# A fused four-layer kernel: the scan's preparation folded in two pieces, keys turned one step later, and unread bf16 matmuls on TensorE in the first part

## The chip, the cores and the metric

The kernel runs on 1 core of one Trainium2 chip. The metric is the device time of one execution in microseconds. The kernel before took 1473.23 us (median of 3 runs, 1469.16 to 1474.96).

## The reference

Eight sequences of 512 tokens with 128 channels go through four layers, each followed by a residual and a layer norm:

```
x = layernorm(x + attention(x))          # 16 heads of 8, causal, q and k layer-normed per head
x = layernorm(x + soft_moe(x))           # 8 experts x 64 slots; softmax over experts (dispatch) and over all slots (combine)
x = layernorm(x + delta_rule_block(x))   # q,k,v = silu(x @ W), l2-normed; recurrent state per head; then a gated MLP
x = layernorm(x + ternary_mlp(x))        # three gelu/silu layers of width 512
```

The first two layers and the preparation of the third (projections, norms, and the folding of four time steps of the delta rule into one) are the first part, up to about 885 us. The scan over time with both MLPs is the second part; the change doesn't touch it.

## The kernel before

The kernel is written by hand, one instruction stream for each engine, with counting semaphores between them. The order of work on each engine is the order in which the code issues it.

The first part is a software pipeline over the 8 sequences. One turn of it is a **slot**, `slot(b, moe, front, tail, ...)`, which works on up to five sequences at once: `b` is in attention (scores, exponentials, products with v), `moe` = b-1 in the expert layer, `front` = b+1 has its q, k, v projected and the maxima of its scores taken, `tail` = b-2 is normed and projected for the third layer, `pre` = b-3 has its heads normed for the scan, and `folded` = b-4 has its time steps folded. So `folded` is there in slots 4 to 7, `front` in slots 0 to 6; slots 3 to 6 are the loop.

Inside a slot the attention's steps `(gg, jt)` (head group, key tile) run from (0, 0) to (4, 3) on TensorE, and the other sequences' work is threaded between them at fixed steps. What matters here, with the lines of the profile:

- **Tops and exponentials of the expert logits.** TensorE makes eight blocks of logits `L0..L3`, `M0..M3` (L962, L966). VectorE takes each one's row maximum (`top`, L1709), and only then can ScalarE take its exponential (L1294, with `accum_out`). L0 to L2 come at the slot's start, L3 and M0 at step (0, 2), M1 and M2 at (0, 3), M3 at (1, 0).
- **`fold_heads`** (VectorE, L1787 to L1807) is a generator of ten steps on the tiles of `late`: products of pairs (L1793, three instructions), a sum (L1796), a fold and a subtraction (L1798, L1799), and two rounds of product, sum, subtraction (L1803, L1805, L1806). `sum_scores` (L1811) follows. In a slot, `finish_heads` runs all of it between the tops L2 and L3. SyncE's queue stores the result to DRAM (`store_heads`, L555) and only behind it replicates the next sequence's q and k (L512, then L517).
- **`norms(front)`** (L1669, L1670, the reciprocal root, L1672) gives `qk_n`. At `QK_TURNED = (1, 3)` TensorE transposes q and k (L871), ScalarE writes each twice (`take_qk_T`: L1294 into `arena` and `hilo`), and GpSimd makes the low parts (L699). ScalarE's `take_products`, on which the products of step (2, 0) wait, comes in step (2, 0) between two exponentials.
- **Maxima.** `scores_for_maxima` works off 22 units of scores of `front` at the slot's end: matmuls of 32 rows (L903) and a bf16 mask added by a matmul of `ident_b` with `mask_qk` (L906). VectorE reduces each unit (L1683). There are two pairs of PSUM banks, so unit k waits until unit k-2 is reduced. Units 14 to 21 are 512 columns wide; units 17 to 21 come behind all other PE work of the slot. Then the maxima are transposed (L871), cast (L1690) and sent by DMA into `qr` (L525), which the next slot's scores need.

`ps` bank 6 holds the attention's products `pvT`; `ring` hands banks 4, 5, 7 to everything else. `idle` matmuls don't exist in this kernel.

Of the kernel before, what the change touches and what calls it, by code (L numbers as in the profile page):

```python
# [21 lines left out]
ACT = mybir.ActivationFunctionType  # L22
X = mybir.AxisListType.X

P = 128
B, S, D = 8, 512, 128
NT = S // P
# [20 lines left out]
CREDIT = 1  # L48
# [93 lines left out]
def build(nc, A, out, taps=None):  # L142
    ctx = ExitStack()
    with ctx:
# [529 lines left out]
        def _(g):  # L674
# [81 lines left out]
            def slot(i, front, pre):  # L756
                for gg in range(NG):
                    for jt in range(NT):
                        if i is not None:
                            causal(i, gg, jt)  # L760
                        if front is not None:
                            if (gg, jt) == (0, 1):
                                squares(front)
                            if (gg, jt) == QK_TURNED:
                                low_parts(front)
                        if pre is not None and (gg, jt) == (2, 1):
                            squares_heads(pre)
                if front is not None:
                    place_v(front)
                    add_bias(front)  # L770
                if pre is not None:
                    scale_heads(pre)
                    score_products(pre)
# [73 lines left out]
        def _(pe):  # L847
# [34 lines left out]

            def transpose_qk(b, turn):
                pe.wait_ge(qk_normed, CREDIT + b + 1)
                transposes("qT", turn, [qk_n[:, t, 0:D] for t in range(NT)]).then_inc(f_ready, 1)
                transposes("kT", turn, [qk_n[:, t, D:2 * D] for t in range(NT)]).then_inc(f_ready, 1)

            def scores_for_maxima(b, first, end):
# [4 lines left out]
                for k in range(first, end):  # L893
# [11 lines left out]
                    for bank in banks:  # L905
                        last = pe.matmul(bank[:, :, it * P:w], ident_b[:, :],  # L906
                                         mask_qk[:, :].unsqueeze(1).broadcast_to([P, len(gs), P]), start=False, stop=True)
                    last.then_inc(s_ready, 1)

            def transpose_maxima(b, turn):  # L910
# [114 lines left out]
            def slot(b, moe, front, tail, before):  # L1025
# [4 lines left out]
                if moe is not None:  # L1030
                    for t in range(3):
                        token_logits(moe, turn, t)
                if b is not None:
                    pe.wait_ge(max_placed, CREDIT + (b + 1) * 64)
                for gg in range(NG + 1):
                    for jt in range(NT):
                        if b is not None and gg < NG:
                            scores(b, gg, jt)
                        if front is not None:
                            if (gg, jt) in ((0, 0), (0, 1)):  # L1040
                                project_qkv(front, turn, 2 * jt)
                                project_qkv(front, turn, 2 * jt + 1)
                            if (gg, jt) == QK_TURNED:
                                transpose_qk(front, turn)
                        if moe is not None:
# [45 lines left out]
                if moe is not None:  # L1091
                    expert_hidden(moe, turn, 2)
                    expert_hidden(moe, turn, 3)
                if tail is not None:
                    transpose_x2(tail, turn)
                if b is not None:
# [25 lines left out]
                if front is not None:  # L1122
                    maxima_to(NX)
                    transpose_maxima(front, turn)
# [11 lines left out]
            turn_weights(6, [raw_slot[:, j, :] for j in range(4)]).then_inc(slot_turned, 1)  # L1136
            transpose_qk(0, first)
            pe.wait_ge(slot_taken, 1)
            scores_for_maxima(0, 0, NX)
            transpose_maxima(0, first)  # L1140
# [140 lines left out]
        def _(act):  # L1281
# [26 lines left out]

            def take_qk_T(b):


                act.wait_ge(split_done, CREDIT + b)
                act.wait_ge(split_stored, CREDIT + b * 96)
                for j, n in enumerate("qk"):
                    for dst in (qk_T[:, j, :], hilo[:, j, 0, :]):
                        r = take(F, f"{n}T", b, dst, lambda p: p, ACT.Identity, scale=qk_gb[:, 2 * j:2 * j + 1],
                                 bias=qk_gb[:, 2 * j + 1:2 * j + 2])
                    r.then_inc(f_act, 1)

# [68 lines left out]
            def slot(b, moe, front, tail):  # L1388
# [5 lines left out]
                for gg in range(NG):  # L1394
                    for jt in range(NT):
# [5 lines left out]
                        if front is not None:  # L1401
                            if (gg, jt) in ((0, 0), (0, 1)):
                                take_qkv(front, 2 * jt)
                                take_qkv(front, 2 * jt + 1)
                            if (gg, jt) == QK_TURNED:
                                take_qk_T(front)
                        if moe is not None:
# [42 lines left out]
            act.wait_ge(w_final, 1)  # L1450
            take_qk_T(0)
            act.wait_ge(setup_pool, 8)
# [127 lines left out]
        def _(v):  # L1580
# [243 lines left out]
            def slot(b, moe, front, tail, pre, folded):  # L1824
                tops = None
                if moe is not None:
                    for t in range(3):
                        top(moe, "L", t)
                    if folded is not None:
                        finish_heads(folded)  # L1830
                    top(moe, "L", 3)
                    top(moe, "M", 0)
                    tops = slot_tops(moe)
                if front is not None:
                    norms(front, (lambda: next(tops, None)) if tops else None)
                if moe is not None:
# [3 lines left out]
                    v.reciprocal(z_inv, z_sum).then_inc(inv_ready, 1)  # L1840
                    apply_x1(moe)
                if b is not None:
                    attend(b, 0)
# [157 lines left out]

QK_TURNED = (1, 3)

# [33 lines left out]
```

## Time and profile before

| | |
|---|---|
| median of 3 runs | 1473.23 us |
| profiled execution, own time | 1466.32 us |
| its span | 1464.6 us |
| busy: PE, DVE, ACT, POOL | 1144.2, 969.0, 618.8, 448.4 us |
| mean granted TensorE clock | 0.84 of full speed |

The profiled execution's time is its span and 1.7 us around it. Durations come from this one execution. The digits of the page's second part give for each fortieth of the span (36.6 us) how busy an engine was, in tenths; PEclk is the clock that TensorE was granted, where 1.00 is 2.4 GHz and 0.50 is 1.2 GHz; in between, a slice holds stretches of both:

```
PE   2778898897988988989897602049898898988997
DVE  3616436564686685866847758888888898888221
PEclk7576797998988979889699755569898989898898
```

### The profile page before, as it was taken

What the parts mean: (1) busy time and instruction counts of PE and PEld (TensorE: products, weight loads), DVE (VectorE), ACT (ScalarE), POOL (GpSimd) and SP (SyncE); (2) the same over time, 40 slices, a digit from 0 to 9 for tenths busy, and PEclk for the clock granted to TensorE, in tenths of its full rate; (3) what the DMA queues carried; (4) which work ended last, traced back from release to release, by engine and by line L of the source; (5) the groups of instructions that cost most, each with busy time, mean ns of one, the idle gap of its engine ahead of it and who ended that gap; (6) DMA issues with size and microseconds to landing.
All of it is one profiled execution on the core that took longest, in us unless ns stands there. A gap on an engine that the chain in (4) does not pass through costs nothing.

```text
span 1464.6 us, 18213 instructions
## 1 busy us (share of the span) xinstructions
PE 1144.2 (78%) x5332; PEld 579.5 (40%) x5332; DVE 969.0 (66%) x2391; ACT 618.8 (42%) x1170; POOL 448.4 (31%) x460
## 2 busy tenths in 40 slices
PE   2778898897988988989897602049898898988997
PEld 1334355453544535535345302014344343443443
DVE  3616436564686685866847758888888898888221
ACT  1061642827537256174374302025344453444542
POOL 2031210302233043341341351153443534435210
PEclk7576797998988979889699755569898988989898
DMA  4111030220322322132103373101022020210000
GB/s 103 65 45 65 1 101 9 59 80 26 104 57 74 87 61 100 40 94 87 35 21 84 83 187 104 45 7 46 8 53 61 8 53 8 53 29 0 22 7 8
DMA packets 85335, 79.83 MB, mean 55 GB/s; under 512 B 42768, under 2 KB 62864, under 8 KB 83216
## 3 DMA queue, kind: packets, MB, share of 16 engines
q1 hardware_dynamic: 85264, 79.01, 19.7%
q8 instruction: 29, 0.48, 0.1%
q14 instruction: 42, 0.34, 0.1%
HBM read 43.45 MB, written 35.00 MB: 54 GB/s over the span
## 4 chain that ended last, share of the span: by engine, by line
PE 61%; DVE 19%; issue 7%; ACT 7%; POOL 2%; SPq 1%; DMA 1%; ACTq 0%; DVEq 0%; POOLq 0%
PE ps L1192 14%; PE ps L1178 9%; PE ps L871 5%; PE ps L933 5%; PE ps L903 5%; DVE arena L1683 4%; PE ps L906 3%; PE ps L922 3%; ACT arena L1332 3%; PE ps L962 2%; PE ps L1184 2%; PE ps L982 2%; ACT arena L1294 2%; PE ps L992 2%; PE ps L966 2%
## 5 line engine op out<-in xcount | busy, mean ns | idle before, releaser
L1294 ACT ACTIVATE arena<-ps 128x512 f32<-128x512 f32 (+2 forms) x200 | 110.1, 573 | 333.4 <-PE ps L871 213.6
L1683 DVE TENSOR_REDUCE arena<-ps 128x2 f32<-128x1024 f32 (+3 forms) x176 | 194.9, 1125 | 56.2 <-PE ps L906 53.5
L1192 PE MATMUL ps<-arena,late 128*128 128x512 f32 x512 | 225.6, 592 | 0.0
L1332 ACT ACTIVATE arena<-ps 128x1024 f32<-128x1024 f32 (+3 forms) x256 | 169.9, 716 | 34.3 <-PE ps L922 32.5
L721 POOL TENSOR_SCALAR_AFFINE_SELECT arena<-arena 128x512 f32<-128x512 f32 x128 | 86.2, 676 | 299.9 <-ACT arena L1332 299.1
L1178 PE MATMUL ps<-arena,late 128*128 128x512 f32 x256 | 135.3, 689 | 12.4 <-ACT arena L1464 12.4
L1192 PEld LDWEIGHTS ps<-arena,late 128*128 128x128 f32 x512 | 96.2, 190 | 115.8 <-issue 115.5
L871 PE MATMUL ps<-ident,arena 128*128 128x128 f32 (+1 forms) x640 | 108.8, 315 | 37.6 <-ACT arena L1294 12.2
L903 PE MATMUL ps<-kr,qr 32*128 32x512 f32 (+3 forms) x512 | 110.2, 481 | 32.3 <-issue 20.1
L1464 ACT ACTIVATE arena<-ps,f_s 128x512 f32<-128x512 f32 x128 | 87.3, 688 | 70.2 <-PE ps L1192 46.4
L933 PE MATMUL ps<-arena 128*32 128x512 f32 (+3 forms) x1024 | 98.2, 468 | 23.0 <-ACT arena L1294 23.0
L798 POOL TENSOR_TENSOR arena<-arena 128x512 f32<-128x512 f32 x64 | 81.3, 1270 | 99.1 <-ACT e_w L1514 99.1
L871 PEld LDWEIGHTS ps<-ident,arena 128*128 128x128 f32 (+1 forms) x640 | 78.9, 155 | 75.4 <-ACT arena L1294 19.7
L1464 ACT ACTIVATE arena<-ps 128x512 f32<-128x512 f32 x96 | 56.2, 597 | 103.2 <-PE ps L1184 70.9
L922 PE MATMUL ps<-qr,kr 32*128 32x256 f32 (+3 forms) x512 | 73.4, 437 | 23.8 <-ACT arena L1332 17.7
L1722 DVE RECIPROCAL arena<-ps 128x16 f32<-128x16 f32 x32 | 8.2, 257 | 122.0 <-PE ps L871 121.5
L1178 PEld LDWEIGHTS ps<-arena,late 128*128 128x128 f32 x256 | 55.2, 222 | 84.3 <-issue 71.5
L903 PEld LDWEIGHTS ps<-kr,qr 32*128 32x128 f32 x512 | 51.9, 227 | 84.7 <-DVE arena L1683 46.4
L922 PEld LDWEIGHTS ps<-qr,kr 32*128 32x128 f32 x512 | 34.1, 193 | 116.7 <-ACT arena L1332 88.9
L1709 DVE TENSOR_REDUCE arena<-ps 128x1 f32<-128x512 f32 x64 | 43.6, 689 | 46.6 <-PE ps L962 35.8
L713 POOL TENSOR_TENSOR arena<-arena,bias_o 128x512 f32<-128x512 f32 x8 | 10.1, 1267 | 208.2 <-DVE arena L1620 208.2
L808 POOL TENSOR_TENSOR arena<-arena 128x512 f32<-128x512 f32 x32 | 40.7, 1273 | 104.3 <-ACT arena L1464 104.2
(164 smaller groups left out, 1978.0 us busy)
## 6 DMA issues: line engine op xcount, KB each, us to landing
scan_d<-late SPq DMA_DIRECT2D x64, 138.0 KB, 2.9
qr<-q_rep SPq DMA_DIRECT2D x8, 1024.0 KB, 5.6
kr<-k_rep SPq DMA_DIRECT2D x8, 1024.0 KB, 7.9
arena<-scan_d SPq DMA_DIRECT2D x12, 552.0 KB, 7.0
q_rep<-hilo SPq DMA_DIRECT2D x24, 256.0 KB, 3.0
k_rep<-hilo SPq DMA_DIRECT2D x24, 256.0 KB, 3.9
proj_d<-arena SPq DMA_DIRECT2D x8, 768.0 KB, 5.1
late<-proj_d SPq DMA_DIRECT2D x8, 768.0 KB, 4.4
```

Of the source, the lines that this page charges most:

```text
L721: g.affine_select(out=block, in_=block, compare_op=ALU.is_ge, fill=0.0, base=0, pattern=[[0, 4], [1, P]], channel_multiplier=-1).then_inc( ...
L798: g.tensor_tensor(o_m[half][r][:, :, :, 0:HD], state[h][:, cs, :, :], qc[:, cs, r, :].unsqueeze(2).broadcast_to([P, HALF, HD, HD]), ALU.mult)
L871: last = pe.transpose(bank[0:src.shape[1], k * P:(k + 1) * P], src, ident[:, :])
L903: pe.matmul(bank[:, j, :], qr[rows, gg, it * P:(it + 1) * P], kr[rows, gg, 0:w], start=(j == 0), stop=False)
L922: last = pe.matmul(ps[:, 2 * (k % 2) + n, 0:S - jt * P], kr[rows, gg, jt * P:(jt + 1) * P], qr[rows, gg, jt * P:S], start=True, stop=True)
L933: last = pe.matmul(bank[32 * h4:32 * h4 + 32, jt * P:S], v_aug[:, jt, 4 * gg + h4, :], prob[:, gg % 2, h4, p_off[jt]:p_off[jt] + S - jt * ...
L1178: return pe.matmul(ps[:, ring2.bank(use), :], w, src, start=True, stop=True)
L1192: last = pe.matmul(ps[:, ring2.bank(f"{n}{c}"), :], w[:, k, c * P:(c + 1) * P], src[:, k, :], start=(k == 0), stop=(k == HC - 1))
L1294: return act.activation(dst, src(ps[:, bank, :]), func, **kw)
L1332: act.activation(prob[:, gg % 2, 2 * pr:2 * pr + 2, p_off[jt]:p_off[jt] + w], ps[:, bank:bank + 2, 0:w], ACT.Exp).then_inc(p_taken, 1)
L1464: return act.activation(dst, src(ps[:, ring2.bank(use), :]), func, **kw)
L1683: v.tensor_reduce(heads[:, 2 * pr:2 * pr + 2, gs[0]:gs[-1] + 1], ps[:, 2 * (k % 2):2 * (k % 2) + 2, 0:len(gs) * w].rearrange("p q (n w) -> ...
```

## The change

Five edits, all in the first part. (1) In slots with `folded`, the first 4 of `fold_heads`' steps stay between the tops L2 and L3; the others and `sum_scores` go behind `apply_x1(moe)`. (2) `QK_TURNED` becomes `Q_TURNED = (1, 3)` and `K_TURNED = (2, 0)`: TensorE, ScalarE and GpSimd do the keys one step later. (3) A helper `idle_matmuls` writes products into `ps` bank 6 that nobody reads: two ahead of each of the units 17 to 21, four ahead of the transposition of the maxima, two ahead of the wait for `max_placed` at a slot's start. (4) The 22 maxima units ahead of slot 0 have two each ahead of them. (5) In the last slot 24 stand ahead of `transpose_x2`.

```diff
                         if front is not None:
                             if (gg, jt) == (0, 1):
                                 squares(front)
-                            if (gg, jt) == QK_TURNED:
+                            if (gg, jt) == K_TURNED:
                                 low_parts(front)
...
-            def transpose_qk(b, turn):
-                pe.wait_ge(qk_normed, CREDIT + b + 1)
-                transposes("qT", turn, [qk_n[:, t, 0:D] for t in range(NT)]).then_inc(f_ready, 1)
-                transposes("kT", turn, [qk_n[:, t, D:2 * D] for t in range(NT)]).then_inc(f_ready, 1)
+            def transpose_qk(b, turn, j):
+                if j == 0:
+                    pe.wait_ge(qk_normed, CREDIT + b + 1)
+                transposes(("qT", "kT")[j], turn, [qk_n[:, t, j * D:(j + 1) * D] for t in range(NT)]).then_inc(f_ready, 1)
...
+            def idle_matmuls(n, bank=6):
+                for _ in range(n):
+                    pe.matmul(ps[:, bank, :], ident_b[:, :], mask_qk[:, :].unsqueeze(1).broadcast_to([P, 4, P]),
+                              start=True, stop=True)
...
                     for t in range(3):
                         token_logits(moe, turn, t)
+                    if b is not None:
+                        idle_matmuls(2)
                 if b is not None:
                     pe.wait_ge(max_placed, CREDIT + (b + 1) * 64)
...
-                            if (gg, jt) == QK_TURNED:
-                                transpose_qk(front, turn)
+                            if (gg, jt) == Q_TURNED:
+                                transpose_qk(front, turn, 0)
+                            if (gg, jt) == K_TURNED:
+                                transpose_qk(front, turn, 1)
...
                 if tail is not None:
+                    if moe is None:
+                        idle_matmuls(24)
                     transpose_x2(tail, turn)
...
                 if front is not None:
-                    maxima_to(NX)
+                    while x_at < NX:
+                        idle_matmuls(2)
+                        maxima_to(x_at + 1)
+                    idle_matmuls(4)
                     transpose_maxima(front, turn)
...
-            scores_for_maxima(0, 0, NX)
+            for k in range(NX):
+                idle_matmuls(2)
+                scores_for_maxima(0, k, k + 1)
             transpose_maxima(0, first)
...
-                            if (gg, jt) == QK_TURNED:
-                                take_qk_T(front)
+                            if (gg, jt) == Q_TURNED:
+                                take_qk_T(front, 0)
+                            if (gg, jt) == K_TURNED:
+                                take_qk_T(front, 1)
...
                     if folded is not None:
-                        finish_heads(folded)
+                        o_fold = Order(v, wy_done, DVE_WY, folded, CREDIT)
+                        folds = fold_heads(folded, o_fold)
+                        advance(o_fold, folds, 4)
                     top(moe, "L", 3)
...
                     apply_x1(moe)
+                    if folded is not None:
+                        advance(o_fold, folds, DVE_WY + 1)
+                        sum_scores(folded)
...
-QK_TURNED = (1, 3)
+Q_TURNED, K_TURNED = (1, 3), (2, 0)
```

## Rows read from the trace of the kernel before

**Rows 1.** Chain of waits in time: starts of slots 2, 3, 4, 5 (start, us)

```profile
243.44 1.88 PE ps L871 x8
333.33 1.88 PE ps L871 x8
...
425.12 1.88 PE ps L871 x8
...
520.75 1.88 PE ps L871 x8
```

**Rows 2.** Timeline of DVE, slot 5: start, duration; brackets: idle before, who ended it

```profile
530.21 0.69 DVE L1803 TENSOR_TENSOR late<-late 128x512 f32<-128x512 f32 x1
...
534.15 2.11 DVE L1806 TENSOR_TENSOR late<-late 128x256 f32<-128x256 f32 x1
536.38 1.49 DVE L1811 TENSOR_REDUCE late<-late 128x160 f32<-128x1280 f32 x1
537.79 1.28 DVE L1709 TENSOR_REDUCE arena<-ps 128x1 f32<-128x512 f32 x2
...
558.01 0.26 DVE L1722 RECIPROCAL arena<-ps 128x16 f32<-128x16 f32 x1 [7.56 <-PE ps L871]
```

**Rows 3.** Timeline of ACT, slot 5

```profile
538.58 0.69 ACT L1294 ACTIVATE arena<-ps,arena 128x512 f32<-128x512 f32 x1 [3.68 <-DVE arena L1709]
...
550.62 0.78 ACT L1294 ACTIVATE arena<-ps,qk_gb 128x512 f32<-128x512 f32 x1
```

**Rows 4.** Timeline of PE, slot 2, then slot 5

```profile
280.53 3.84 PE L982 MATMUL ps<-arena 128*128 128x128 f32 x32
...
533.41 1.13 PE L962 MATMUL ps<-slot_T,arena 128*128 128x512 f32 x2
...
539.41 2.08 PE L966 MATMUL ps<-arena,slot_T 128*128 128x512 f32 x2 [2.70 <-ACT arena L1294]
...
554.93 1.37 PE L933 MATMUL ps<-arena 128*32 128x512 f32 x8 [2.11 <-ACT arena L1294]
...
563.31 3.83 PE L982 MATMUL ps<-arena 128*128 128x128 f32 x32
```

**Rows 5.** Timeline of PE, late units of slot 5; logits at the slot's start

```profile
522.64 3.90 PE L962 MATMUL ps<-slot_T,arena 128*128 128x512 f32 x6
...
605.72 0.50 PE L903 MATMUL ps<-kr,qr 32*128 32x512 f32 x2 [0.40 <-DVE arena L1683]
...
606.85 0.79 PE L903 MATMUL ps<-kr,qr 32*128 32x512 f32 x2 [0.41 <-DVE arena L1683]
607.58 0.39 PE L906 MATMUL ps<-mask_qk,ident_b 128*128 128x128 bf16 x2
```

**Rows 6.** Timeline of DVE, late units of slot 5

```profile
607.74 8.53 DVE L1683 TENSOR_REDUCE arena<-ps 128x2 f32<-128x1024 f32 x7
```

**Rows 7.** Chain of waits: two bf16 matmuls of 512 columns, unit 0 and slot 5

```profile
45.06 0.96 PE ps L906 x2
...
584.30 0.54 PE ps L906 x2
```

**Rows 8.** Windows: PE, PEld, DVE, ACT, POOL busy (x), PEclk, DMA share, GB/s

```profile
43.90:72.60 28.70, 25.97 (x108) 11.30 (x108) 24.31 (x22) 0.00 (x0) 0.00 (x0) 0.50 0.00 1
...
606.80:620.40 13.60, 11.80 (x39) 5.63 (x40) 11.54 (x15) 1.20 (x2) 11.02 (x10) 0.50 0.07 20
```

**Rows 9.** Timeline of SP's queue, slot 5

```profile
538.05 4.72 SPq L555 DMA_DIRECT2D scan_d<-late  x8
555.87 1.88 SPq L512 DMA_DIRECT2D q_rep<-hilo  x3
...
572.17 0.40 SPq L517 DMA_DIRECT2D qr<-q_rep  x1
```

**Rows 10.** Timeline of ACT, slot 7

```profile
729.79 0.69 ACT L1294 ACTIVATE arena<-ps,arena 128x512 f32<-128x512 f32 x1 [4.44 <-DVE arena L1709]
```

**Rows 11.** Timeline of PE, slot 9

```profile
835.86 1.11 PE L871 MATMUL ps<-ident,arena 128*128 128x128 f32 x4 [9.40 <-DVE arena L1620]
```

More of the change, by code:

```diff
@@ L1136, in _ @@
             turn_weights(6, [raw_slot[:, j, :] for j in range(4)]).then_inc(slot_turned, 1)
-            transpose_qk(0, first)
+            transpose_qk(0, first, 0)
+            transpose_qk(0, first, 1)
             pe.wait_ge(slot_taken, 1)
-            scores_for_maxima(0, 0, NX)
+            for k in range(NX):
+                idle_matmuls(2)
+                scores_for_maxima(0, k, k + 1)
             transpose_maxima(0, first)
@@ L1307, in take_qkv, with take_qk_T @@
                 act.activation(v_new[:, t, :], ps[:, ring.bank(f"qkv{t}"), 2 * D:3 * D], ACT.Copy).then_inc(f_act, 1)
[L1309 to L1318, printed above, removed]
+            def take_qk_T(b, j):
+                if j == 0:
+                    act.wait_ge(split_done, CREDIT + b)
+                    act.wait_ge(split_stored, CREDIT + b * 96)
+                for dst in (qk_T[:, j, :], hilo[:, j, 0, :]):
+                    r = take(F, ("qT", "kT")[j], b, dst, lambda p: p, ACT.Identity, scale=qk_gb[:, 2 * j:2 * j + 1],
+                             bias=qk_gb[:, 2 * j + 1:2 * j + 2])
+                r.then_inc(f_act, 1)
             def exponential(b, gg, jt, pr):
@@ L1450, in _ @@
             act.wait_ge(w_final, 1)
-            take_qk_T(0)
+            take_qk_T(0, 0)
+            take_qk_T(0, 1)
             act.wait_ge(setup_pool, 8)
```

## The prediction

> **What bounds the kernel now.** I read the page first: PE is busiest, yet its PEclk digits dip again and again in the first part, which in a pipeline of many short waits says that the order of the engines' work, not their sum, sets the pace. So the second view is the chain of waits in order of time. Each slot begins with the same piece, the transposes behind the last maximum, and their starts give the slot lengths [rows 1]: slot 2, with no folding, takes 333.33 - 243.44 = 89.9 us; slot 4, with folding, 520.75 - 425.12 = 95.6 us (5 and 6 are its repetitions in the loop). The reader is to look for where the 5.7 us go.
>
> Third, the timelines of one folding slot. In slot 5 VectorE folds behind L2's top, comes to the second half at 530.21 and has the sum at 536.38 + 1.49 = 537.9 [rows 2]. TensorE had L3's logits by 533.41 + 1.13 = 534.5 [rows 4], but their top comes only at 537.79 [rows 2]; ScalarE stands 3.68 us for it, and TensorE 2.70 us behind ScalarE [rows 3, 4]. After this wait TensorE runs at 1.2 GHz for a while: 2.08 us for one block of logits that took 1.13 us before. A second stall stands at 554.93: 2.11 us, ended by ScalarE [rows 4]. There ScalarE has first worked off the four activations of the turned q and k, 0.78 us each, from 550.62 on [rows 3], before it frees the product bank. From the slot's start to the gathering matmuls (L982) it is 563.31 - 520.75 = 42.6 us in slot 5 and 280.53 - 243.44 = 37.1 us in slot 2 [rows 1, 4].
>
> Fourth, the slot's end: seven reductions of 1024 columns follow each other in 8.53 us, 1.22 us each [rows 6]. VectorE sets the pace and TensorE waits for it. TensorE's clock falls at about 606.8, although it worked up to there with waits of only 0.40 and 0.41 us [rows 5], and stays at 0.50 up to 620.4, in the next slot [rows 8].
>
> **The change, part by part.**
>
> *Folding in two pieces.* The first four steps end where L1803 starts, at 530.21 [rows 2]. That is 4.3 us ahead of L3's logits, so the top of L3 is no longer late. The slot then goes as slot 2 goes up to L982: 42.6 - 37.1 = 5.5 us less in each of slots 4 to 6, together 16.5 us. What is late next there is ScalarE, which is busy almost without a gap from L3's exponential to the second step of head group 2, as in slot 2; I count nothing beyond slot 2's pace.
>
> The removed half comes back behind `apply_x1`. From 530.21 to 537.87 it took 7.7 us, 1.7 of them in one subtraction that took 2.11 us [rows 2] against 0.42 us for most of its kind: 6.0 us without it. VectorE stood idle for 7.56 us there, up to 558.01 [rows 2]: it fits with 1.6 us to spare. Queued behind it is `attend(b, 0)`, for whose bank TensorE waits. What could use up the spare: the long subtraction ran beside a multiplication of GpSimd's, and GpSimd's low parts, now a step later, fall into the new place. One such collision costs 1.7 us, so I take 0 and keep 0 to 2 us per slot, 8 us over four slots, for the range. Here the Trainium skill ("SBUF — State Buffer", section "SBUF: two separate sides") says that VectorE and GpSimd share a port pair as an exclusive lock, so that the later one waits for the other's whole instruction. The trace agrees with its one long subtraction; by the rule the worst case is one whole low-parts instruction per slot, which lies inside that same range.
>
> SyncE's stores move with the sum: from 538.05 to about 551, 4.72 us of issue, so the six replications that stand behind them are issued from about 555.5 as before [rows 9], while the rest of the slot is 5 us earlier. The load that needs them comes at 572.17 [rows 9], then at about 567; they take 3.8 us to issue and some 4 to land, to 563.5. Cost 0 with 3 us to spare; without it one to three us per slot.
>
> In slot 7 there is no `front`. ScalarE stands 4.44 us for the same top [rows 10], of which about 1 us is TensorE's slow logits: 3.5 us.
>
> *Keys a step later.* ScalarE reaches `take_products` up to 2 x 0.78 = 1.6 us sooner [rows 3], but does the same work in all. The transposes of the next step now wait for the key copies, so most of it returns. What is kept is that the 2.11 us stall splits in two and the clock is less likely to fall. In folding slots that is in the 5.5 already. Slot 3, without folding, took 425.12 - 333.33 = 91.8 us, 1.9 us more than slot 2 [rows 1]; slots 1 and 3 may get 1 us each: 2 us. The bounds are 0 and 4 us. GpSimd and SyncE get the keys 2 us later, inside the 3 us above.
>
> *Unread matmuls at the slot's end.* No row shows one. By the nearest, the mask matmuls of the same operands and 512 columns, a pair costs 0.54 us at 2.4 GHz and 0.96 us at 1.2 GHz [rows 7]. A unit takes about 0.73 us to its end at 2.4 GHz (0.50 us of scores from 605.72, then the mask, partly beside them) and 606.85 to 607.97 = 1.12 us at 1.2 GHz [rows 5]. They stand ahead of a unit in TensorE's queue. At 2.4 GHz pair and unit make 1.27 us by these rows against the reduction's 1.22 us [rows 6], and the next pair starts before the unit's last results are out: 0. At 1.2 GHz they make 2.08 us: each of the five units is 0.86 us late, and VectorE can't catch up.
>
> The gain: with the clock up, the transposes and the first logits of the next slot (3.90 us for three blocks, part of them slow [rows 5]) are quicker, but VectorE first casts, adds and adds again before it can take L0's top, which leaves 1.0 us. The bounds per slot: -1.0 us (clock up all through) and 5 x 0.86 - 0 = +4.3 us (never up; less about 1 us if the four matmuls ahead of the transposes bring it back in time: +3.3). Since the clock fell before the first of the new pairs stands [rows 5], I take it that it comes back after about two units: 1.8 - 1.0 = +0.8, rounded to +1 for each of the seven slots 0 to 6: +7 us.
>
> The Trainium skill ("TensorE: Matmul & The Clock Gate", section "Step-by-step: what each phase is for") says that only weight loads are pulled ahead, matmuls keep the order of the program. It speaks against this edit: an unread matmul can't step aside for a late unit. By it the pair's full 0.96 us stands on the path wherever TensorE is late, which is the +4.3 us case; the rows fit it, as the units in them never overtake.
>
> *The maxima ahead of slot 0.* 28.7 us, clock 0.50, VectorE busy 24.31 us [rows 8]. Clock up: -3 us. Clock never up: 21 pairs of 0.96 us added to TensorE, which was busy 25.97 us and so is the bound: 25.97 + 20.2 - 28.7 = +17 us. I take 0: a few slow units at first, and then the gain of the quick ones, since 20 of the units come after the first pairs.
>
> *The 24 in the last slot.* TensorE stood 9.40 us [rows 11]; at 0.54 us a pair they take 6.5, at 0.96 us 11.5 us. 0; bounds -1 and +2.
>
> *Sum:* -16.5 - 3.5 - 2 + 7 + 0 + 0 = -15 us. The profiled execution took 1466.32 us, so 1451 us by its own time. The median of the runs stands 6.9 us above it; on it the same sum gives 1458 us.
>
> **The rivals.**
>
> *The clock stays up all through.* -1 instead of +1 per slot and -3 ahead of slot 0: -16.5 - 3.5 - 2 - 7 - 3 = -32, 1441 us. For it: the pairs are full-array work in what was waiting. Against: in slot 5 the clock is down before the first pair.
>
> *The clock doesn't come back in the late units (the other side).* TensorE then becomes the bound of the maxima: 7 x 3.3 + 17 - 22 = +18, 1491 us. The point from which it decides: above +3.1 us per slot with slot 0's units at a loss of 0, or half the units slow there. For it: TensorE was busy 11.80 of 13.60 us at 0.50 and didn't come back [rows 8]. Against: that work was of 32 rows mostly.
>
> *The folding's gain is given back* by the port, by `attend(b, 0)` or by the replications: half of the 22 us lost, -11 + 7 = -4, 1469 us. For it: 1.6 and 3 us to spare are little. Against: VectorE's next work absorbs about 1 us.
>
> **How the numbers follow.** Forecast 0.50, own range 1450 to 1466; clock up 0.20; clock down 0.17; gain given back 0.13. A measurement of this kernel can tell about 0.5%, 7.4 us, from no change, so faster is below 1465.9 and slower above 1480.6. Faster: 0.47 of the forecast, 0.20, and 0.05 of the last: 0.72. Slower: 0.16. Same: 0.12. The range reaches from 1438 to 1484 us: it holds most of the clock-up case and leaves out most of the clock-down case.
>
> **What would show it.** Right: slots 4 to 6 near 91 us between the first transposes; ScalarE's wait ahead of L3's exponential below 1 us; SyncE's L555 in folding slots some 10 us after its old place, L512 not. The reductions of units 17 to 21 further apart than 1.22 us for two units, then 1.22. Wrong: L1683 at 2 us intervals up to unit 21 (clock down), or a PEclk of 1.00 in that stretch (clock up); a long L1803 to L1811 beside L699 with a late L1722 (given back). If slots 4 to 6 stay above 93 us without slow late units, the first step of the sum fails.

## The result, and the profile after

The changed kernel took 1453.3 us (median of 4 runs) against 1474.1 us for the kernel before (4 runs): ratio 0.987, interval 0.984 to 0.991. In a later comparison (12 runs against 25) it was 0.9915, 0.988 to 0.995. Faster in both, by 0.9 to 1.3%; the forecast was 1458 us and -15 us. The profiled executions took 1466.32 and 1453.12 us: 13.2 us less.

Where these went is read from the gathering matmuls, a fixed place in every slot. The chain of waits of the kernel before has them at (start, us; duration; what):

```profile
189.95 3.83 PE ps L982 x32
280.54 3.83 PE ps L982 x32
372.04 3.83 PE ps L982 x32
467.74 3.83 PE ps L982 x32
563.31 3.83 PE ps L982 x32
658.88 3.83 PE ps L982 x32
748.99 3.83 PE ps L982 x32
```

and the same view of the changed kernel, slots 1 to 7 (L982 is now L988):

```profile
190.15 3.83 PE ps L988 x32
285.72 3.83 PE ps L988 x32
380.04 3.83 PE ps L988 x32
469.51 3.83 PE ps L988 x32
561.17 3.83 PE ps L988 x32
649.44 3.83 PE ps L988 x32
735.85 3.83 PE ps L988 x32
```

The steps between them were 90.6, 91.5, 95.7, 95.6, 95.6, 90.1 us and are 95.6, 94.3, 89.5, 91.7, 88.3, 86.4 us. So the first two steps got longer by 5.0 and 2.8 us, and the next four shorter by 6.2, 3.9, 7.3 and 3.7 us; slot 1's gathering itself came 0.2 us later: +7.8 - 21.1 + 0.2 = -13.1 us. From slot 7's gathering to the end nothing changed (715.6 us in both).

Inside a folding slot the forecast's signs are there. VectorE, slot 5 of the changed kernel (timeline: start, duration; in brackets the idle time before and who ended it; L1709 is now L1730, L1722 L1743, L1811 L1832):

```profile
532.84 0.42 DVE L1820 TENSOR_TENSOR late<-late 128x256 f32<-128x256 f32 x1
537.80 0.69 DVE L1730 TENSOR_REDUCE arena<-ps 128x1 f32<-128x512 f32 x1 [4.53 <-PE ps L968]
...
548.18 0.69 DVE L1824 TENSOR_TENSOR late<-late 128x512 f32<-128x512 f32 x1
...
552.68 1.49 DVE L1832 TENSOR_REDUCE late<-late 128x160 f32<-128x1280 f32 x1
555.80 0.26 DVE L1743 RECIPROCAL arena<-ps 128x16 f32<-128x16 f32 x1 [1.64 <-PE ps L871]
```

VectorE now waits 4.53 us for L3's logits instead of making them wait, and the second half of the folding, 548.18 to 554.17, has 1.64 us to spare before the product bank comes: the forecast had 6.0 us of work and 1.6 us to spare. ScalarE stands 0.48 us ahead of L3's exponential, against 3.68 [rows 3]:

```profile
538.60 0.69 ACT L1312 ACTIVATE arena<-ps,arena 128x512 f32<-128x512 f32 x1 [0.48 <-DVE arena L1730]
```

TensorE's stall of 2.11 us [rows 4] is split in two, and its first logits take 2.81 us instead of 3.90 [rows 5]:

```profile
526.82 2.81 PE L968 MATMUL ps<-slot_T,arena 128*128 128x512 f32 x6 [0.32 <-DVE arena L1711]
...
552.93 1.06 PE L939 MATMUL ps<-arena 128*32 128x512 f32 x8 [0.76 <-ACT arena L1312]
...
555.11 1.14 PE L871 MATMUL ps<-ident,arena 128*128 128x128 f32 x8 [0.73 <-ACT hilo L1312]
```

SyncE's queue has the stores 29.0 us behind the slot's first transposes (17.3 before) and the replications 33.8 us behind them (35.1 before) [rows 9]: moved as forecast, and in this slot TensorE has no wait for the load that needs them.

```profile
554.35 4.73 SPq L555 DMA_DIRECT2D scan_d<-late  x8
559.18 2.31 SPq L512 DMA_DIRECT2D q_rep<-hilo  x3
```

The late units come in two kinds. The timeline of VectorE, first slot 1, then slot 5 (L1683 is now L1704):

```profile
240.22 1.23 DVE L1704 TENSOR_REDUCE arena<-ps 128x2 f32<-128x1024 f32 x1 [0.68 <-PE ps L906]
242.12 1.23 DVE L1704 TENSOR_REDUCE arena<-ps 128x2 f32<-128x1024 f32 x1 [0.68 <-PE ps L906]
...
605.57 8.00 DVE L1704 TENSOR_REDUCE arena<-ps 128x2 f32<-128x1024 f32 x7
```

and the windows over these two stretches (us, then busy time of PE, PEld, DVE, ACT, POOL; PEclk; DMA share, GB/s):

```profile
235.00:249.00 14.00, 13.73 (x46) 5.78 (x46) 9.05 (x9) 0.60 (x1) 1.27 (x1) 0.51 0.06 19
603.00:615.00 12.00, 10.03 (x56) 4.12 (x54) 11.30 (x15) 0.68 (x2) 9.12 (x9) 1.00 0.07 22
```

In slot 1 the clock fell at 235.1, ahead of the first pair, and never came back in the units: 1.90 us each, with TensorE as the bound. In slot 5 it stayed at 1.00: 1.14 us each, less than the 1.22 of before. Slots 1, 2 and 4 went the first way (from the gathering to the start of the last reduction 55.8, 54.8 and 54.5 us, before 51.5 to 52.2), slots 3, 5 and 6 the second (51.2 to 51.3). Slot 0 went a third way: its last reductions stand 2.06, 1.40 and then 1.14 us apart, as the clock came back.

### The profile page after: what moved, and what is told of

The parts are those of the page before. It is cut to its first block, busy times and chain, and to the rows that moved or that the text cites. A ratio compares the mean times of both kernels' runs of the same rounds, so it can differ in the third digit from the quotient of the medians.

```text
span 1451.4 us, 18572 instructions
## 1 busy us (share of the span) xinstructions
PE 1154.9 (80%) x5512; PEld 582.6 (40%) x5512; DVE 964.3 (66%) x2391; ACT 617.7 (43%) x1170; POOL 448.7 (31%) x460
## 4 chain that ended last, share of the span: by engine, by line
PE 59%; DVE 18%; ACT 9%; issue 8%; POOL 3%; DMA 2%; SPq 1%; ACTq 0%; DVEq 0%; POOLq 0%
PE ps L1210 14%; PE ps L1196 9%; PE ps L871 4%; PE ps L903 4%; ACT arena L1350 4%; PE ps L939 4%; DVE arena L1704 4%; PE ps L906 3%; ACT arena L1312 3%; PE ps L928 3%; PE ps L1202 2%; PE ps L988 2%; PE ps L913 2%; PE ps L998 2%; PE ps L1006 2%
## 5 line engine op out<-in xcount | busy, mean ns | idle before, releaser
L1704 DVE TENSOR_REDUCE arena<-ps 128x2 f32<-128x1024 f32 (+3 forms) x176 | 194.3, 1124 | 67.5 <-PE ps L906 66.2
L871 PE MATMUL ps<-ident,arena 128*128 128x128 f32 (+1 forms) x640 | 103.9, 303 | 33.1 <-ACT arena L1312 12.2
L903 PE MATMUL ps<-kr,qr 32*128 32x512 f32 (+3 forms) x512 | 98.7, 435 | 26.8 <-DMA kr<-k_rep 19.4
L798 POOL TENSOR_TENSOR arena<-arena 128x512 f32<-128x512 f32 x64 | 81.0, 1266 | 99.3 <-ACT e_w L1535 99.3
L871 PEld LDWEIGHTS ps<-ident,arena 128*128 128x128 f32 (+1 forms) x640 | 75.2, 149 | 74.0 <-issue 20.4
L1196 PEld LDWEIGHTS ps<-arena,late 128*128 128x128 f32 x256 | 55.2, 222 | 84.2 <-issue 71.4
L903 PEld LDWEIGHTS ps<-kr,qr 32*128 32x128 f32 x512 | 47.5, 210 | 95.6 <-DVE arena L1704 44.1
L1730 DVE TENSOR_REDUCE arena<-ps 128x1 f32<-128x512 f32 x64 | 43.8, 688 | 51.1 <-PE ps L968 46.3
L1743 DVE RECIPROCAL arena<-ps 128x16 f32<-128x16 f32 x32 | 8.2, 257 | 99.4 <-PE ps L871 99.0
L1179 PE MATMUL ps<-ident,arena 128*128 128x128 f32 x128 | 24.9, 342 | 60.6 <-ACT arena L1485 30.8
```

The lines of the kernel that those rows point to most:

```text
L798: g.tensor_tensor(o_m[half][r][:, :, :, 0:HD], state[h][:, cs, :, :], qc[:, cs, r, :].unsqueeze(2).broadcast_to([P, HALF, HD, HD]), ALU.mult)
L871: last = pe.transpose(bank[0:src.shape[1], k * P:(k + 1) * P], src, ident[:, :])
L903: pe.matmul(bank[:, j, :], qr[rows, gg, it * P:(it + 1) * P], kr[rows, gg, 0:w], start=(j == 0), stop=False)
L1196: return pe.matmul(ps[:, ring2.bank(use), :], w, src, start=True, stop=True)
L1704: v.tensor_reduce(heads[:, 2 * pr:2 * pr + 2, gs[0]:gs[-1] + 1], ps[:, 2 * (k % 2):2 * (k % 2) + 2, 0:len(gs) * w].rearrange("p q (n w) -> ...
```

## The experiments

All ratios are to the kernel before, run beside each kernel on the same chip; e1 to e8 ran on one chip, e9 to e12 on another. A ratio and the two medians can differ by some us (for e7 -20 us by its ratio, -16 between the medians). The times spread: where the unread matmuls stand, runs of one kernel reached from 1447 to 1475 us (e5), while e1's six lay within 2.2 us; the profiled runs show the clock's falls at other places in each, so a single profile shows a mechanism and not a median. In the profiles of e1 and e9 the stretch behind slot 8's gathering, which holds none of the edits but the 24 matmuls of the last slot, took 660.7 and 660.6 us, in the twelve others 663.3 to 664.0: 3 us of these two kernels' profiled gains stand where their edits change nothing. Theory A is the sum on record; A2 is its successor after the first four runs: the folding's wait and the low clock at the slots' starts are largely one loss, which either edit takes away.

**e1, the folding alone.**

```diff
-                        finish_heads(folded)
+                        advance(o_fold, folds, 4)
...
                     apply_x1(moe)
+                    if folded is not None:
+                        advance(o_fold, folds, DVE_WY + 1)
+                        sum_scores(folded)
```

> The kernel before with one edit: the first four steps of fold_heads stay between the tops L2 and L3, the others and sum_scores go behind apply_x1. Theory A (the sum on record): this edit alone is worth 5.5 us in each of slots 4 to 6 and 3.5 us in slot 7, so about 1474 - 20 = 1454 us; the way from slot 4's first transposes to its gathering matmuls falls from 42.6 to about 37.1 us. Rival B (part of the gain seen is the clock's, brought by the unread matmuls): 1458 us or more, the same way still 39 us or more. In both the maxima at each slot's end stay as they were, 51.7 us from the gathering to the last reduction.

Measured: 1455.3 us, ratio 0.9925 (0.991 to 0.994), which is -11 us, half of the 20. The slot that the expectation names, slot 4, did go as theory A says, 430.83 to 468.08 us in the chain of waits, 37.25 us:

```profile
430.83 1.90 PE ps L871 x8
...
468.08 3.83 PE ps L988 x32
```

From 436.0 to 514.5 us, in its late units, its clock stayed at 1.00. In slots 5 and 6 it fell again ahead of the gathering (552.1 to 555.5 and 644.2 to 647.6 us at 0.50), and they took 38.7 us. TensorE in slot 6 (timeline):

```profile
612.56 1.88 PE L871 MATMUL ps<-ident,arena 128*16 128x128 f32 x8 [1.32 <-DVE arena L1697]
614.45 4.04 PE L968 MATMUL ps<-slot_T,arena 128*128 128x512 f32 x6
...
642.85 1.07 PE L939 MATMUL ps<-arena 128*32 128x512 f32 x8 [2.10 <-ACT arena L1305]
```

From the transposes to the gathering at 651.28 it is 38.7 us: 3.9 us less than before, not 5.5. And two slots that hold no folding became slower: from the start of the previous slot's last reduction to the gathering, slots 2 and 3 took 40.7 and 40.6 us, against 38.4 and 40.0 before. The clock falls elsewhere there (268.8 to 279.0, 330.2 to 343.9 and 360.9 to 367.8 us at 0.50). The 37.1 us that the prediction took from slot 2 were not the pace of a slot without folding, but of one that happened to run at a clock of 1.00 from 248.4 to 326.9 us, as slot 4 of e1 did.

**e2, the folding and the keys, no unread matmul.** e1's edit with e4's:

```diff
-QK_TURNED = (1, 3)
+Q_TURNED, K_TURNED = (1, 3), (2, 0)
```

> The changed kernel without any unread matmul: folding in two pieces and keys a step later. Theory A (unread matmuls cost on balance): in the changed kernel's trace the last reduction came 3.6, 3.3 and 2.7 us late in slots 1, 2 and 4, 0.5 us early in slots 3, 5 and 6, and 4.4 us late up to slot 0's end, 12 us in all, of which the quicker starts of the slots give some 5 back; without them 1453 - 7 = 1446 us, and below e1 by the 0 to 4 us of the keys. Rival B (they pay): 1456 us or more.

Measured: 1454.5 us, 0.9925 (0.9905 to 0.994). Both theories miss: the changed kernel's two ratios, 0.987 and 0.9915, are lower, but the second not by what a measurement can tell; and the keys add nothing to the folding that it can tell.

**e3, the unread matmuls alone.** The kernel before with all calls of `idle_matmuls`:

```diff
+                        idle_matmuls(2)
+                    idle_matmuls(4)
+                    idle_matmuls(2)
+                        idle_matmuls(24)
+                idle_matmuls(2)
```

> The kernel before with all unread matmuls and nothing else. Theory A: a cost, 1474 + 7 = 1481 us, with 1.9 us between the reductions of a slot's last units wherever the granted clock is 0.50 there, and 1.14 us where it is 1.00. Rival B: 1467 us or less, since the folding slots start at a clock of 1.00.

Measured: 1452.9 us, 0.9905 (0.987 to 0.994), single runs from 1444 to 1467 us. Theory A falls: the unread matmuls alone are worth 14 us, no less than the folding's 11. In the profiled run they cost 15.6 us ahead of slot 0, where the clock never rose and a unit with its pair took 1.90 us (VectorE's last two of 22 reductions, and the window over the stretch):

```profile
85.13 1.23 DVE L1704 TENSOR_REDUCE arena<-ps 128x2 f32<-128x1024 f32 x1 [0.68 <-PE ps L906]
87.03 1.23 DVE L1704 TENSOR_REDUCE arena<-ps 128x2 f32<-128x1024 f32 x1 [0.68 <-PE ps L906]
```

```profile
43.90:88.60 44.70, 43.24 (x152) 16.43 (x153) 24.82 (x22) 0.00 (x0) 0.00 (x0) 0.50 0.00 1
```

In the kernel before, also at 0.50 but without pairs, the last reduction started at 71.4 us. All of the loss was won back: from slot 3 on its steps from gathering to gathering were 90.3, 89.0, 89.0 and 86.4 us (before 95.7, 95.6, 95.6 and 90.1), with the folding where it was. In slot 5, at a clock of 1.00, ScalarE stands only 1.85 us ahead of L3's exponential. The line names TensorE's L972, whose block ended at 544.40; L3's top, which the exponential needs, came from VectorE in the reductions from 543.64 on:

```profile
544.44 0.69 ACT L1312 ACTIVATE arena<-ps,arena 128x512 f32<-128x512 f32 x1 [1.85 <-PE ps L972]
```

The slot's first reductions come sooner behind quicker logits, the folding starts sooner, and the stall leaves no slow logits behind it. From the start of the last reduction to the gathering it is 37.8 us in each of slots 4 to 6: 6.1 less than before (43.8), while the folding edit on top of it saves another 0.7 (37.1 in slots 5 and 6 of the changed kernel).

Not all of the 6.1 us is TensorE's clock. The folding's subtraction takes 0.43 us instead of 2.11 [rows 2]:

```profile
541.69 0.43 DVE L1827 TENSOR_TENSOR late<-late 128x256 f32<-128x256 f32 x1
```

GpSimd's multiplication (L694) starts at 541.78, 0.09 us behind it. In the kernel before the order was the other way round, in slots 4, 5 and 6 alike: the multiplication at 534.09, the subtraction 0.06 us behind it, at 534.15. Whichever came second was the slower one: the subtraction by 1.7 us there, the multiplication by 0.2 us here (2.10 against 1.90). e7 has this order in all three slots too, with 0.42 us. So 1.7 of the 6.1 us turn on a start a tenth of a microsecond earlier or later.

**e4, the keys alone.** The line shown at e2 and nothing else.

> The kernel before with the keys turned a step later and nothing else. Theory A: 0 to -4 us, so 1470 to 1474 us; the wait of 2.11 us ahead of the third product step splits into two below 1 us each. Rival: it costs, because low_parts and the keys' replications come later while the folding is still ahead of them: 1476 us or more.

Measured: 1461.3 us, 0.996 (0.9935 to 0.998), so -3 to -10 us, its middle beyond the bound of -4. The stall splits into 0.77 and 0.73 us as expected, and the folding slots' starts are 1.5 to 2.2 us shorter. Beside the folding edit (e2 against e1) no difference is left that the runs can tell.

**e5, the changed kernel again**, beside the next three.

> The changed kernel once more, beside the next three on one chip. With the terms of the earlier runs (folding alone 0.9925, unread matmuls alone 0.9905 with times from 1444 to 1467 us) theory A2 says the two are largely substitutes: both make the slots' starts quick, so together about 0.987 and not 0.983; a spread of several us from the maxima ahead of slot 0, where the granted clock is 1.00 in some executions and 0.50 in others.

Measured: 0.9915 (0.988 to 0.995), 12 runs from 1447 to 1475 us. A2's figure of 0.987 was too good by 0.45%; both comparisons together leave 0.9 to 1.3%.

**e6, no pairs ahead of slot 0.**

```diff
             for k in range(NX):
-                idle_matmuls(2)
                 scores_for_maxima(0, k, k + 1)
```

> The changed kernel without the 22 pairs of unread matmuls ahead of slot 0 (those at the slots' ends and in the last slot stay). Theory A2: the maxima ahead of slot 0 go back to 25.3 us between first and last reduction (27.1 in the changed kernel's trace, about 41 in e3's), the slots keep their gain: 1442 to 1448 us, a narrower spread, 0.980 to 0.985. Rival (the sum on record, in which the pairs ahead of slot 0 cost nothing): as e5, within 3 us.

Measured: 0.991 (0.988 to 0.994), 1457.7 us: the same as e5. A2's gain did not come. Its reductions ahead of slot 0 were indeed over 3.1 us sooner (72.0 against 75.1 us in e5), but e3's loss of 15 us is the worst of three profiled executions with these pairs (+2.1, +3.7 and +15.6 us against before); how often it comes isn't known. On the median 0 was a fair value for this term.

**e7, unread matmuls in the slots only**, with the old folding and keys: e3 with e6's edit.

```diff
-                idle_matmuls(2)
                 scores_for_maxima(0, k, k + 1)
```

> The kernel before with the unread matmuls at the slots' ends and in the last slot, and neither the folding, the keys nor the pairs ahead of slot 0. Theory A2: the slots' gain of e3's trace (21 us from slot 1's gathering to the end) stays whole and e3's loss ahead of slot 0 goes: 1445 to 1450 us, 2 to 4 us above e6, so the folding is worth only 2 to 4 us once the clock is up. Rival (folding worth 11 us by itself, as without unread matmuls): e7 is 8 us or more above e6.

Measured: 0.986 (0.983 to 0.990), 1451.2 us, 6 runs from 1443 to 1464 us. It isn't above e6 by 8 us, but below it: with unread matmuls in the slots the folding and the keys are worth nothing that these spreads can tell. e1 and e7 together are the double count: 11 and 16 to 20 us alone, 10 to 13 us together in e6, which holds both edits and the keys (11 to 21 us in the changed kernel).

**e8, the same unread matmuls over 32 rows.**

```diff
-                    pe.matmul(ps[:, bank, :], ident_b[:, :], mask_qk[:, :].unsqueeze(1).broadcast_to([P, 4, P]),
+                    pe.matmul(ps[:, bank, :], ident_b[0:32, :], mask_qk[0:32, :].unsqueeze(1).broadcast_to([32, 4, P]),
```

> e6's kernel with each unread matmul over 32 rows of its operands in place of 128: the same columns, places and durations on TensorE, a quarter of the array at work. Theory A2 (the gain is the clock's): the granted clock falls in the late units as in the kernel before, the pairs run at 0.96 us there, so 5 x 0.7 us and more are lost per slot; 1465 to 1480 us. Rival C (the gain comes from the delay or the order that the pairs bring, not from the clock): as e6, within 3 us.

Measured: 0.996 (0.994 to 0.998), 1462.8 us. Both figures miss: it is 5 us above e6 (the intervals just touch) and 5 us above e2, which has no unread matmul at all, but 2 us below the 1465 of A2. In the late units of every slot from 1 to 6 the clock stood at 0.50 (1.2 GHz), for 13.6 to 17.1 us, in e6's profile in two of these six only. It fell close to the first pair, between 1.8 us before it and 1.3 us after it, and it stayed down although TensorE was busy all the time (window from the end of slot 5's units into slot 6):

```profile
616.00:622.00 6.00, 5.99 (x15) 2.72 (x15) 3.52 (x5) 0.60 (x1) 2.87 (x4) 0.50 0.01 4
```

TensorE's timeline in the late units shows what else differs:

```profile
611.60 0.60 PE L913 MATMUL ps<-mask_qk,ident_b 32*128 32x512 bf16 x1
611.60 0.79 PE L903 MATMUL ps<-kr,qr 32*128 32x512 f32 x2
```

Both start at 611.60. The pair uses rows 0 to 31; the units use rows 0 to 63 and rows 64 to 127 in turn, and their reductions stand 1.71 and 1.29 us apart in turn, 1.5 us on average against e6's 1.90. So matmuls on different rows of the array run side by side (the Trainium skill, "TensorEngine Tiling (Array Packing)", section "Key Properties", says that different tiles of the array can run matmuls in parallel; the trace agrees). With the smaller delay this kernel is still slower: its pairs cost 0.4% against e2, which has none. That the full rows work through the clock is the reading that fits both the profiles and the times. Rival C falls.

**e9, unread matmuls at the ends only.** e6 without the pairs between units 17 and 21.

```diff
                     while x_at < NX:
-                        idle_matmuls(2)
                         maxima_to(x_at + 1)
                     idle_matmuls(4)
```

> e6's kernel without the pairs between units 17 to 21; the four ahead of the transposed maxima and the two after the first logits stay. Theory A2: the gain of the unread matmuls needs the clock up through the late units; without the pairs the clock falls there as in the kernel before, the units take 1.22 us each (51.7 us from gathering to last reduction) and the slots' starts are slow: as without any unread matmul (e2, 0.9925), within 0.3%. Rival D (the four at the end bring the clock back in time, and the pairs between the units only cost): 0.987 or less.

Measured: 1447.6 us, 0.986 (0.983 to 0.988): rival D's number, and A2's 0.9925 misses by 0.7%. In slot 4's end VectorE sets the pace again and the four follow at the low clock:

```profile
503.47 8.52 DVE L1702 TENSOR_REDUCE arena<-ps 128x2 f32<-128x1024 f32 x7
```

```profile
510.52 1.91 PE L913 MATMUL ps<-mask_qk,ident_b 128*128 128x512 bf16 x4
512.23 1.91 PE L871 MATMUL ps<-ident,arena 128*16 128x128 f32 x8
514.15 2.02 PE L968 MATMUL ps<-slot_T,arena 128*128 128x512 f32 x4
```

The clock is back at 514.3 us, 2.1 us behind the transposes' start, against 4.1 us in slot 5 of before (520.75 [rows 1] to 524.8). The four run in time in which TensorE would wait for the last reduction anyway. From gathering to gathering its steps from slot 1 to slot 6 take 90.0 to 91.5 us: never the 88.3 of a slot at 1.00, never the 91.7 to 95.6 of one that lost the clock with pairs in it.

**e10, pairs also ahead of units 14 to 16.**

```diff
-                maxima_to(X1 + 2)
+                while x_at < X1 + 2:
+                    if front is not None:
+                        idle_matmuls(2)
+                    maxima_to(x_at + 1)
```

> e6's kernel with pairs also ahead of units 14 to 16. Theory A2: where the clock falls, it often falls just ahead of unit 17 (515.0 us in the changed kernel's trace), so the earlier pairs keep more slots at the length seen with the clock up, 88.3 us, and fewer at 91 to 95: 3 to 8 us less than e6, 0.983 to 0.989. Rival (the falls come from the middle of the slot, where TensorE waits for ScalarE): as e6, 0.991, within 0.2%.

Measured: 1447.8 us, 0.9845 (0.982 to 0.987), five runs within 5 us. A2's ratio holds; 3 to 8 us less than e6 were expected, and it is 10, in another comparison. e9, which has no pairs between the units at all, does as well, so that what these pairs add over it isn't shown.

**e11, and a pair ahead of the scores of steps (0, 1), (0, 2) and (0, 3).**

```diff
+                        if b is not None and front is not None and (gg, jt) in ((0, 1), (0, 2), (0, 3)):
+                            idle_matmuls(2)
                         if b is not None and gg < NG:
                             scores(b, gg, jt)
```

> e10's kernel with a pair of unread matmuls also ahead of the scores of the first head group's steps 1 to 3, where TensorE waits 0.67 and 0.47 us for ScalarE. Theory A2: the stretch between a slot's first logits and its gathering keeps the clock at 1.00 more often, 1 to 4 us less than e10. Rival (each pair stands on the path there, at 0.54 us): 3 pairs x 7 slots x 0.3 us, up to 6 us more than e10.

Measured: 1439.2 us, 0.980 (0.977 to 0.982), five runs from 1438.6 to 1440.5 us. 8.6 us below e10, where 1 to 4 were expected, and the best kernel of this case: 2.0% faster than before. Its steps are 89.3, 88.7, 91.2, 88.5, 88.5 and 86.6 us. Between the two profiles 4.9 of 8.4 us come before slot 1's gathering: in slot 0 e10's last reductions stand 1.90 us apart, e11's 1.14. TensorE in slot 5 (timeline):

```profile
517.74 0.59 PE L913 MATMUL ps<-mask_qk,ident_b 128*128 128x512 bf16 x2
518.57 0.44 PE L928 MATMUL ps<-qr,kr 32*128 32x384 f32 x2 [0.24 <-ACT arena L1354]
519.49 0.44 PE L928 MATMUL ps<-qr,kr 32*128 32x384 f32 x2 [0.47 <-ACT arena L1354]
```

This pair, the one of step (0, 1), lies inside the 0.67 us for which TensorE waited for ScalarE in the changed kernel too: it costs nothing. Those of steps (0, 2) and (0, 3) stand in no wait, but what they delay is made up at later waits: from slot 5's first logits to its gathering it is 34.4 us in e11 and in e10. The windows over the same 457 us, slots 2 to 6 in the main, show the clock: the kernel before, the changed one, and e11, one fence each.

```profile
243.00:700.00 457.00, 401.48 (x2583) 215.73 (x2584) 299.60 (x650) 238.12 (x444) 123.11 (x130) 0.90 0.24 70
```

```profile
243.00:700.00 457.00, 413.86 (x2708) 220.56 (x2708) 306.45 (x664) 238.00 (x445) 129.88 (x135) 0.95 0.24 70
```

```profile
243.00:700.00 457.00, 414.21 (x2783) 219.75 (x2782) 314.20 (x674) 245.62 (x458) 134.04 (x143) 0.99 0.25 72
```

**e12, one unread matmul per late unit.** In e6's kernel:

```diff
                     while x_at < NX:
-                        idle_matmuls(2)
+                        idle_matmuls(1)
```

> e6's kernel with one unread matmul instead of two ahead of each of the units 17 to 21. At a clock of 0.50 a unit then takes 1.12 + 0.43 = 1.5 us instead of 1.9, so a slot that has lost the clock loses 1.7 us instead of 3.6; theory A2: if one is enough to keep the clock, 2 to 4 us less than e6 and a narrower spread; if not, the slots fall back to the length of e2 and the median to 0.9925.

Measured: 1454.9 us, 0.9895 (0.987 to 0.992): as e6, within the spreads. In its profile, which was the slowest of its four runs (1461.9 us), one wasn't enough: the clock was at 0.50 for 10.2 to 13.6 us around every slot's end from slot 1 on, and a unit there took the 1.5 us expected (its reductions at 521.54 and 523.01 us).

## Why the prediction was right, and which terms were not

The sum, -15 us, met -13.2 us between the profiles and -11 to -21 us between the medians. Term by term, from the changed kernel's trace, and then from the runs that hold one edit alone:

*Folding in two pieces.* On record -5.5 us for slots 4 to 6, with -1 for their quick starts. Measured from last reduction to gathering: -5.7, -6.6 and -6.8 us. As a length this is right, and so are its parts: top no longer late, second half in VectorE's idle time with 1.6 us to spare, stores moved by 12 us without harm. As a cause it failed. The step that failed is "the slot then goes as slot 2 goes": slot 2's 37.1 us held a clock of 1.00. By e1 the folding alone brings 5.4 us where the clock stays up (slot 4), 3.9 us where it falls (slots 5 and 6), and 11 us in all; by e3 the unread matmuls alone bring 6.1 us with the folding left where it was, 1.7 of them by the subtraction. They overlap, and the folding on top of the unread matmuls is 0.7 us in these profiles. The collision with GpSimd, 0 on record, didn't come: no subtraction of the changed kernel's slots took over 0.43 us, and the low parts began at 555.14 in slot 5, 1.0 us behind the second half. A whole low-parts instruction takes 2.4 us (2.36 in slot 5), so the 2 us a slot that the prediction kept for it in the range were a little too few. Slot 7: -3.5 and -1 on record, -3.2 measured; e1 had -1.0 there and e3 -3.2, so this too comes with the unread matmuls and not with the folding.

*Keys a step later.* On record 0 to -4. Alone -6 us (e4, -3 to -10), beside the folding 0 (e2): inside the bounds of 0 to -4 beside the folding, outside them alone, and again an overlap.

*Unread matmuls at the slot's end.* The mechanism on record was half right. "It comes back after about two units", +1.8 us of late part in every slot, is slot 0's case alone: in slots 1 to 6 the clock either held (late part -0.5 us) or was away for all five units (+3.6, +3.3, +2.7 us, inside the bound of +4.3). The two kinds have a mean of +1.3 us, which is near the record by chance. The term's sign was wrong: +7 us on record; alone -14 us with the pairs ahead of slot 0 (e3), -16 to -20 us without (e7), and beside folding and keys -1 to -8 us (the changed kernel's two ratios against e2's; the first of these can't be told from 0). What was mis-sized is the quick start, -1.0 us on record: it is 2.5 us (37.5 us in slots 4 to 6 of the changed kernel against 40.0 in e2, which lacks the unread matmuls alone), and it also reaches the slots without folding (in e3 slots 1 to 3 start 2.8, 0.9 and 0.7 us quicker than before). What was right is the price of a late unit at the low clock, read from the mask matmuls: 0.96 us a pair [rows 7], 1.90 us a unit seen against 2.08 reckoned.

*Ahead of slot 0.* On record 0, bounds -3 and +17. Seen: +2.1 in the changed kernel, +15.6 in e3, and no difference between the medians of e5 and e6 that the spreads can tell.

*The 24 in the last slot.* On record 0. They took 5.3 us, inside the wait, and the transposes behind them came 13.1 us sooner than before (822.73 against 835.86 us), as did slot 8's gathering: 0. No run has them alone.

The Trainium skill ("TensorE: Matmul & The Clock Gate", section "Step-by-step: what each phase is for") was used against this edit, that no matmul steps aside; the trace agrees in slots 1, 2 and 4, where TensorE has hardly a gap (busy 13.73 of 14.00 us). e9 points to its price: without the pairs between the units the ratio is 0.5% lower than e6's. But the intervals just touch, the two ran on different chips, and 3 us of e9's profile stand where the edit doesn't reach.

So the total was right by luck, because two errors cancelled: folding and keys were counted at -22 us and measured -11 (e2), the unread matmuls at +7 and measured -1 to -8. The rival "the clock stays up all through" (1441 us) came true only in slots 3, 5 and 6, and with pairs in more places in e11: -32 us on record, -30 us there.

One reading of the prediction was also wrong: it says against the rival of a low clock that TensorE's work at 0.50 "was of 32 rows mostly". Of the 11.80 us busy [rows 8] the matmuls of 32 rows were 4.75.

What stays open: what the folding is worth in e11's kernel wasn't run, and the runs don't tell e5, e6 and e12 apart, nor e9 and e10.

## What to carry to other kernels

When a slot is compared with a "clean" one to price a wait, compare the granted clock of the two stretches too: here the clean slot owed 1.6 of its 5.5 us to the clock, by slots 5 and 6 of e1. Two edits that each shorten the same stretch need a run each, and one together; neither's gain is to be read off the kernel that holds both. Unread matmuls pay where the engine waits anyway: ahead of ScalarE's results (e11), or while the last reduction runs (e9). Put between units for which TensorE is the bound once the clock has fallen, each pair delays real work at half speed (1.90 us a unit instead of 1.22).

## What the runs showed of the hardware

The clock fell although TensorE was hardly ever idle: it was busy 11.80 of 13.60 us at 0.50 [rows 8], 4.75 of them in matmuls of 32 rows, with waits of about 0.4 us before [rows 5], and in e8 it stayed down with TensorE busy 5.99 of 6.00 us. The Trainium skill ("TensorE: Matmul & The Clock Gate", section "HAM oscillation — how this bites in real kernels") looks for long idle stretches as the cause; by that section these units would have kept the clock. e8 against e6 says that the rows which the matmuls use count: with the same columns over 32 rows the clock fell in all of slots 1 to 6, over 128 rows it stayed down through the units of slot 1 alone and was back after two in slot 3. That is one profile each, and in two of e8's six slots the fall came ahead of the first pair; the medians, 5 us apart, point the same way. Full rows are no guarantee either: in slot 1 of the changed kernel the clock stayed down with pairs over 128 rows and TensorE busy 13.73 of 14.00 us.

VectorE and GpSimd slowed each other when they started within 0.1 us: the subtraction took 2.11 us when it started 0.06 us behind the multiplication, and 0.43 us when it started 0.09 us ahead (before and e3).

And one kernel's executions differ by up to 28 us (e5); its two profiles differ in the places of the clock's falls. Filling the stretches ahead of them (e11) took 2% off the time, and its five runs agree within 2 us. A narrow spread alone doesn't show that the clock is up, though: the six runs of e1, without any unread matmul, lie within 2.2 us.
